# Whole fp32 operands in place of three products on split parts, in layer 1's second feed-forward product and output projection

## What is computed

```
xn  = layernorm(x)
ctx = attention context of 32 heads of 16, 8 groups       # 1024 x 512
h   = gelu(xn @ inter_w + inter_b)                        # 1024 x 2048
x   = x + (ctx @ Wo + bo) + (h @ output_w + output_b)     # 1024 x 512
```

## Time and profile before

| | us |
|---|---|
| median of 3 runs | 1771.76 |
| lowest, highest run | 1762.22, 1773.39 |
| span of the profiled execution | 1769.7 |
| its own time beside the span | not given |
| PE busy in the span | 1668.8 (94%) |
| DVE, ACT, POOL busy | 1089.3, 849.2, 708.5 |

### The profile page before, as it was taken

One profiled execution on the slowest core, in us unless ns is written; L12 is line 12 of the kernel. 1 busy time (PEld: TensorE's weight loads), 2 busy tenths in 40 slices (PEclk: granted clock), 3 DMA queues, 4 the chain that ended last, 5 costly groups with the idle time before them and its releaser, 6 DMA issues. The chain is left out here.

```text
span 1769.7 us, 27326 instructions
## 1 busy us (share of the span) xinstructions
PE 1668.8 (94%) x8874; PEld 1226.8 (69%) x8874; DVE 1089.3 (62%) x2491; ACT 849.2 (48%) x1595; POOL 708.5 (40%) x735
## 2 busy tenths in 40 slices
PE   6899998999989999999999999789999999999998
PEld 5688887888766666666666666477765555568887
DVE  3556658999747777776777776335657677510222
ACT  3456556443326555555555555344135565653321
POOL 1112213444647566665566665386001111222221
PEclk9999999999999999999999999899979999999999
DMA  7522323220200001000001000364532343131111
GB/s 244 167 73 85 95 84 83 59 66 22 77 13 1 19 19 37 19 19 19 19 19 37 19 19 13 98 203 140 159 48 50 64 81 64 45 98 62 48 48 48
DMA packets 110717, 114.16 MB, mean 65 GB/s; under 512 B 39521, under 2 KB 71745, under 8 KB 110593
## 3 DMA queue, kind: packets, MB, share of 16 engines
q1 hardware_dynamic: 108288, 108.40, 21.8%
q10 hardware_dynamic: 2304, 4.20, 0.6%
HBM read 83.97 MB, written 28.44 MB: 64 GB/s over the span
## 5 line engine op out<-in xcount | busy, mean ns | idle before, releaser
L1490 POOL TENSOR_SCALAR a_p<-a_p,a_rinv 128x640 f32<-128x640 f32 (+7 forms) x256 | 190.6, 748 | 172.6 <-DVE a_rinv L1416 171.6
L1447 ACT ACTIVATE a_p<-a_sm,a_nmax 128x640 f32<-128x640 f32 (+7 forms) x256 | 198.6, 777 | 111.6 <-DVE a_nmax L1408 109.1
L1408 DVE CUSTOM_DVE_ANT_0 a_sm<-ps,maskb 128x640 f32<-128x640 f32 (+7 forms) x256 | 192.5, 752 | 94.7 <-PE ps L1352 91.2
L2334 DVE CUSTOM_DVE_ANT_0 ga_sm<-ps,strip 128x640 f32<-128x640 f32 (+1 forms) x224 | 163.2, 754 | 78.8 <-PE ps L2241 77.3
L2354 ACT ACTIVATE ga_pt<-ps 128x1024 f32<-128x1024 f32 (+1 forms) x192 | 148.1, 810 | 114.8 <-PE ps L2264 114.1
L1364 PE MATMUL ps<-ident,a_p 128*128 128x128 f32 x1152 | 172.1, 274 | 10.6 <-DVE a_pt L1423 10.4
L1364 PEld LDWEIGHTS ps<-ident,a_p 128*128 128x128 f32 x1152 | 132.9, 140 | 33.6 <-issue 10.5
L2394 POOL TENSOR_SCALAR_AFFINE_SELECT ga_pt<-ga_pt 128x512 f32<-128x512 f32 x64 | 40.6, 634 | 286.5 <-ACT ga_pt L2354 286.5
L1379 PE MATMUL ps<-a_pt,vst 128*64 128x512 f32 (+3 forms) x768 | 152.4, 506 | 1.8 <-DVE a_pt L1423 1.1
L1459 ACT COPY a_pt<-ps 128x512 f32<-128x512 f32 x128 | 74.2, 580 | 151.8 <-PE ps L1364 100.0
L1352 PE MATMUL ps<-kh,lq_qh 128*128 128x512 f32 (+3 forms) x384 | 131.7, 397 | 15.4 <-DVE a_nmax L1408 10.6
(11 more groups left out here) (319 smaller groups left out, 3972.1 us busy)
## 6 DMA issues: line engine op xcount, KB each, us to landing
ctx_d<-a_ctxst SPq DMA_DIRECT2D x16, 512.0 KB, 2.9
idx<-ctx_d SPq DMA_DIRECT2D x32, 256.0 KB, 3.8
idx<-wvo_d SPq DMA_DIRECT2D x32, 256.0 KB, 4.5
ga_qst<-qkd SPq DMA_DIRECT2D x42, 128.0 KB, 4.2
f_wr<-in_L_ffn_w SPq DMA_DIRECT2D x18, 256.0 KB, 2.7
x<-in_L_attn_hidden_states SPq DMA_DIRECT2D x16, 256.0 KB, 3.9
op_wo<-in_L_attn_o_w SPq DMA_DIRECT2D x8, 512.0 KB, 4.5
ix_w<-in_L_attn_idx_wq_w SPq DMA_DIRECT2D x64, 64.0 KB, 1.9
```

The source lines that it names most:

```text
L1408: dve.tensor_tensor_reduce(out=sm[kind][:, 0:w], in0=slots[kind][:, 0:w], in1=maskb[:, MASK_OFF[t]:MASK_OFF[t + 1]], scale=-scale, scalar= ...
L1447: act.activation(p[kind][:, v // 2 % 2, 0:w], sm[kind][:, 0:w], ACT.Exp, bias=nmax[:, v % 4:v % 4 + 1], scale=-1.0, accum_out=rsum[:, v % ...
L1490: pool.tensor_scalar(mine, mine, rinv[:, v % 4:v % 4 + 1], 1.0, ALU.mult, ALU.mult).then_inc(norm_done, 1)
L2334: dve.tensor_tensor_reduce(out=sm[kind][:, 0:w], in0=slots[kind][:, 0:w], in1=strip[:, S - w:], scale=-1.0, scalar=3.0e38, op0=ALU.add, op ...
```

## The change

The down stage multiplies the fp32 operands as they are: the stationary operand is `whole(i)` and the moving one `w2r`, one call of `matmul` in place of the three of `mm3`. All that made the parts goes: `high_g`, `high2`, `low2`, VectorE's subtraction, the buffers `w2h`, `w2l`, `gh`, `gl`, and five semaphores. `down(i)` waits for the landing of its weights and for both Gelus of its block, or for the scaled context. A buffer of the ring `w2r` is loaded anew once PE has used it (`used`). The up stage is unchanged. The core of the diff:

```diff
                 def second(i):
                     if i >= RW:
-                        sp.wait_ge(w2l_done, START + i - RW + 1)
+                        sp.wait_ge(used, START + i - RW + 1)
...
                 def down(i):
-                    hi, lo = parts(i)
-                    pe.wait_ge(w2l_done, START + i + 1)
-                    pe.wait_ge(gl_done, START + i + 1)
+                    pe.wait_ge(w2_in[i % RW], START + 16 * (i // RW + 1))
+                    if i < NC:
+                        pe.wait_ge(h_done, START + 2 * i + 2)
+                    else:
+                        pe.wait_ge(rest["norm_done"], START + G1 // 2)
                     for t in ((4, 5, 6, 7, 0, 1, 2, 3) if i == 0 else range(ST)):
                         at = slice(t * P, (t + 1) * P)
                         if i == 0 and t < 4:
                             pe.wait_ge(h_done, START + 2 * (NC - 2) + t + 1)
-                        ins = mm3(pe, ps[:, t, :], (hi[:, at], lo[:, at]), (w2h[:, i % RW], w2l[:, i % RW]), i == 0,
-                                  i == NK - 1)
+                        ins = pe.matmul(ps[:, t, :], whole(i)[:, at], w2r[:, i % RW], start=i == 0, stop=i == NK - 1,
+                                        skip_group_check=True)
...
-                def high2(i):
-                    act.wait_ge(w2_in[i % RW], START + 16 * (i // RW + 1))
-                    if i >= RW:
-                        act.wait_ge(used, START + i - RW + 1)
-                    act.copy(w2h[:, i % RW], w2r[:, i % RW]).then_inc(w2h_done, 1)
...
-                def high_g(i):
-                    if 1 <= i <= DT:
-                        act.wait_ge(hidden, START + 2 * NC)
-                    elif i > DT:
-                        act.wait_ge(used, START + i - DT + 1)
-                    if i < NC:
-                        act.wait_ge(h_done, START + 2 * i + 2)
-                    else:
-                        act.wait_ge(rest["norm_done"], START + G1 // 2)
-                    act.copy(parts(i)[0], whole(i)).then_inc(gh_done, 1)
...
                 for k in range(NC):
                     if k + 2 < NC:
                         high1(k + 2)
-                    elif k == NC - 2:
-                        high_g(0)
-                        high2(0)
-                    else:
-                        high2(1)
-                        high2(2)
                     activate(k)
-                for i in range(1, NK):
-                    high_g(i)
-                    if i + 2 < NK:
-                        high2(i + 2)
...
-                for i in range(NK):
-                    low2(i)
...
-                for i in range(NK):
-                    hi, lo = parts(i)
-                    dve.wait_ge(gh_done, START + i + 1)
-                    dve.tensor_tensor(lo, whole(i), f32(hi), ALU.subtract).then_inc(gl_done, 1)
```

More of the change, by code:

```diff
@@ L120 @@
                 exp_done=2)
-LAYER1 += names("t_", "bias_in bias_done x_ready w2h_done w2l_done h_done gh_done gl_done used summed x_done stored",
+LAYER1 += names("t_", "bias_in bias_done x_ready h_done used summed x_done stored",
                 w1_in=2, w2_in=4)
@@ L2418, in heads_and_ffn @@
         w2r = c.sb("t_w2r", [P, RW, D])
[L2419 to L2422, removed]
         bias = c.sb("t_bias", [P, 2, D])
-        names = ("bias_in", "bias_done", "x_ready", "w2h_done", "w2l_done", "h_done", "gh_done", "gl_done", "used", "summed", "x_done", "stored")
-        (bias_in, bias_done, x_ready, w2h_done, w2l_done, h_done, gh_done, gl_done,
-         used, summed, x_done, stored) = (c.sem("t_" + n) for n in names)
+        names = ("bias_in", "bias_done", "x_ready", "h_done", "used", "summed", "x_done", "stored")
+        (bias_in, bias_done, x_ready, h_done, used, summed, x_done, stored) = (c.sem("t_" + n) for n in names)
         w1h_done, w1l_done, hidden, b1, b1_in = (ahead[n] for n in ("high", "low", "hidden", "b1", "b1_in"))
@@ L2433, in bank @@
             return 2 * (k % 2) + half + (4 if k < 2 else 0)
[L2435 to L2439, removed]
         def whole(i):
```

## The result

The kernel after takes 1798.56 us (median of 4 runs, 1793.93 to 1804.87), the kernel before 1772.58 us (4 runs). The ratio is 1.0151, with a 95% interval of 1.0108 to 1.0195: slower by 1.5%, some 26 us. Forecast were 1801.4 us and slower by 1.7%.

What follows compares the result with a forecast made beforehand. PE alone was taken to bound the second product: 320 x 0.436 = 139.5 us against 109.9, +29.6, all else zero. Span 1769.7 + 29.6 = 1799.3, with 2.1 more 1801.4 us; range 1789 to 1812.

Steps and rivals of the forecast that it cites:

- What bounds the stage: Second product: PE alone bounds it, 109.9 us for 480 matmuls; removing work from the other three engines cannot shorten it.
- third rival: Second product: preparation on shared memory costs PE 15.6 ns a pass, which vanishes; within 1% by some saving; chance 3%.
- Two instructions a product, two passes each: Second product: 320 fp32 matmuls replace 480, each streaming 512 columns at two cycles a column; 0.86 against 0.687 us a product.
- composition from narrower products: Full-width fp32 price inferred from line 1379's tiles of 64 and line 2280's of 32, which fill the array for 0.43 us.
- The addition per instruction: Second product: small extra per fp32 instruction beyond 427 ns streaming; 436 ns taken, ends 427 and 458.
- the 442 and 458 of the forecast: Nanoseconds per fp32 instruction in the second product: 427 plus the fp32r pass's 15.6 paid once, or twice (high end).
- Loads hidden: Second product: each fp32 weight load, at most 0.11 us, hides behind a 427 ns stream and costs nothing.
- first rival: Second product: PE cannot hide fp32 weight loads, 0.11 us more per instruction, 174.7 us, +64.8, time 1836.6; chance 3%.
- The other engines, the waits, the tail: Down stage: removed roundings and subtractions, new waits for loads and Gelus, and the final addition and store change nothing: zero.
- The time: Whole kernel: span 1799.3 us plus 2.1 to the median gives 1801.4 us, 1.7% slower.

## Why the prediction was right

*What bounds the stage.* Right. The stage has PE busy throughout, 110.00 of 110.00 us before and 137.40 of 137.40 after, at a granted clock of 1.00 both times; taking the preparation away without touching the number of matmuls gives a ratio of 0.9993. The third rival (splitting hindered PE) was given a weak argument in the prediction: its up stage has VectorE nearly idle, but ScalarE and GpSimd as busy as the down stage has them. The stretch from 1746 us on, with all three nearly or wholly idle and still 228.8 ns a matmul, is the stronger one, and was in the same trace.

*Two instructions a product, two passes each.* Right: 320 matmuls, 0.429 us each, never two within a slot. The composition from narrower products held and is now shown at this place by the run with two tiles of 64. The price of 0.86 us a product was the prediction's (0.858 measured).

*The addition per instruction.* This is the term that was mis-sized. The text put 436 ns, the middle between the rows' 430 for fp32 tiles and 442, which took over the 15.6 ns of the fp32r pass. Measured are 429.2: fp32 has its own addition of 2.6 ns per instruction, the same with 256 and with 512 columns, and the 15.6 ns were seen with fp32r operands only. The 213.3 ns under the 15.6, and with it the 442 and 458 of the forecast and the last digit of the 427 (the rows have 0.43 us), were an assumption of the author's: no row of the kernel before shows them. The runs gave the number afterwards, as 429.2 - 215.9 for 256 columns of fp32, and put 215.9 beside it for 512 of bf16. The sum was to be 139.5 us and is 137.4, so +27.5 in place of +29.6. The row that had the right type (430 ns on line 1379) was nearer than the row that had the right width.

*Loads hidden.* Right, so the first rival (+64.8) fell. All operands here have 128 rows, the loads of 0.19 us (188 to 190 ns) start while a matmul streams, and PE loses nothing by them: it takes 429.2 ns an instruction with 512 columns, and 215.9 with 256, where a load comes twice as often.

*The other engines, the waits, the tail.* Right at zero. The last Gelu:

```profile
L2511 ACT ACTIVATE t_g<-ps,ah_b x32: 680/687/702, 1571.4 to 1650.0; 128x512 f32<-128x512 f32 x32
```

It starts at 1650.0, 0.2 us into the down stage, and tile 0 needs it only 3.4 us in. The final additions now wait for PE one by one, as forecast:

```profile
1785.62 0.69 DVE L2542 TENSOR_TENSOR x<-ps,x 128x512 f32<-128x512 f32 x1 [0.17 <-PE ps L2488]
...
1786.48 0.69 DVE L2542 TENSOR_TENSOR x<-ps,x 128x512 f32<-128x512 f32 x1 [0.17 <-PE ps L2488]
1787.34 0.69 DVE L2542 TENSOR_TENSOR x<-ps,x 128x512 f32<-128x512 f32 x1 [0.17 <-PE ps L2488]
```

The last starts with the end of PE and takes 0.69 us, and the span ends 4.9 us after its start, as before (1769.7 - 1764.76 = 4.9).

*The time.* 1798.6 against 1801.4, within the range. 2.1 us of the 2.8 are the mis-sized term. That the rest is so small is partly luck. The span was forecast at 1799.3 and is 1792.2, of which 4.9 us are the earlier arrival of this execution; and the median lies 6.4 us above that span, where the forecast put 2.1, taken from one profiled execution before. The two nearly cancel (-4.9 and +4.3). The stage, +27.5 against +29.6, is what tests the reasoning.

## What to carry to other kernels

Before replacing several products on parts by one on whole operands, count passes, not instructions: here whole fp32 takes the time of four passes of the moving columns (0.858 us), three products on parts take three (0.687 us), and where PE is the bound and the splitting is hidden behind it, the fewer passes win by 0.17 us per 128 x 128 x 512 product on fp32r parts. If a product must be priced before it exists in a trace, look for a row with the same type of operands as well as one with the same shape: here the type gave the nearer price, and column tiles that fill the array together (0.43 us a pair) showed the full-width cost (0.429 us an instruction). Where parts are kept, a matmul on bf16 parts takes 6% less than one on fp32r parts here (215.9 against 228.9 ns); what the sum loses in precision is not shown. When a run that makes neighbours idle is faster, look in the kernel before for a stretch where they are idle anyway, before calling them the cause.

## What was not expected of the hardware

An fp32r matmul of 512 columns takes 228.9 ns where bf16 takes 215.9, though both are counted as one pass. Of the 13 ns between them, idle neighbours (228.8) and alternating banks (228.9) give back nothing, other buffers for the stationary operand 2 (226.8), and halving that operand under 1 (228.3); halving the moving one leaves 11.2 of the 15.6. What is left is tied to the type and partly to the columns. Whether the reading of four-byte values alone makes it, and why fp32, which also has four bytes a value but takes two passes (429.2 ns), is free of it, stays open: no run had an fp32r operand on one side only.
